# Gated blocks stored through ScalarE's DMA queue instead of SyncE's, in a language adapter with temporal gating

## The reference, cut to what matters

```python
# stage 0: adapter chosen by the sequence's language, residual, layer norm
h  = relu(x @ W1[lang] + b1[lang]);  a = h @ W2[lang] + b2[lang]
x1 = x + layernorm(x + a) * gamma0 + beta0
# stage 1
ctx    = causal_ema(x1, tau_ctx)                           # over positions
gated  = x1 * sigmoid(concat([x1, ctx]) @ Wg.T + bg)       # called g in the kernel
mod    = 0.5 + sigmoid(gelu(x1 @ Wn1.T + bn1) @ Wn2.T + bn2)   # 8 factors a position
traces = [causal_ema(gated * mod[..., d], tau[d]) for d in range(8)]
temporal = sum over d of traces[d] * softmax(blend)[d]
gate = sigmoid(temporal @ Wtemp.T + btemp)
soma = gelu(x1 @ Wsoma.T + bsoma)
out  = x1 + layernorm((soma * gate) @ Wout.T) * gamma + beta
```

## Time and profile before

| what | value |
|---|---|
| median of 3 runs | 1540.48 us (1540.35 to 1543.76) |
| the profiled execution: its time | 1546.37 us |
| its span | 1544.6 us |
| granted TensorE clock over the span | 0.988 |
| PE busy | 1430.2 us (93%) |
| DVE busy | 1004.6 us (65%) |
| ACT busy | 466.4 us (30%) |
| POOL busy | 398.0 us (26%) |
| DMA queue q1 (all DMAs of the program) | 184.97 MB, 41.0% of 16 engines |

### The profile page before, as it was taken

The page is one execution under the profiler, slowest core; times in us unless marked ns, Lnnn a source line. Parts: engine busy times, 40 slices in busy tenths (PEclk is TensorE's granted clock), DMA queues, the critical chain, the costliest instruction groups (busy, mean ns, idle before and its releaser), DMA issues.

```text
span 1544.6 us, 18784 instructions
## 1 busy us (share of the span) xinstructions
PE 1430.2 (93%) x7532; PEld 911.1 (59%) x7532; DVE 1004.6 (65%) x1421; ACT 466.4 (30%) x723; POOL 398.0 (26%) x294
## 2 busy tenths in 40 slices
PE   2899999999999999999899998999999999999986
PEld 1555756566575655756566575655756566575643
DVE  6866666765766666666765766666666765766362
ACT  2323332332323323332332332323332332333321
POOL 4304132240422304232230422304132140421102
PEclk8899999999999999999999999999999999999998
DMA  6471542616236261452516344271542616243150
GB/s 209 165 194 55 152 122 91 189 48 170 83 116 168 80 162 55 147 160 90 156 42 181 112 120 133 79 193 55 149 124 89 191 43 176 83 121 97 54 138 28
DMA packets 66137, 186.18 MB, mean 121 GB/s; under 512 B 9090, under 2 KB 13826, under 8 KB 53762
## 3 DMA queue, kind: packets, MB, share of 16 engines
q1 hardware_dynamic: 66050, 184.97, 41.0%
HBM read 134.61 MB, written 50.33 MB: 120 GB/s over the span
## 4 chain that ended last, share of the span: by engine, by line
PE 34%; DMA 28%; DVE 23%; SPq 5%; issue 4%; ACT 2%; POOL 1%; POOLq 0%; DVEq 0%
DMA g_spans<-g 21%; PE ring L784 20%; PE ring L791 12%; DVE U L694 9%; DMA grep<-g_spans 6%; DVE x L676 6%; SPq L308 5%; DVE U L667 2%; DVE seq_lo L621 2%; PE Tp L922 1%; PE Tp L912 1%; DVE g L706 1%; DVE V L712 1%; ACT g L460 1%; DVE g L702 1%
## 5 line engine op out<-in xcount | busy, mean ns | idle before, releaser
L694 DVE TENSOR_TENSOR U<-grep,w_qs 128x1024 f32<-128x1024 f32 x256 | 297.6, 1220 | 116.3 <-DMA grep<-g_spans 116.0
L363 POOL TENSOR_TENSOR x<-grep,b_row 128x512 f32<-128x512 f32 x64 | 83.3, 1333 | 673.2 <-DMA grep<-in_x 673.2
L784 PE MATMUL ring<-Wout,soma 128*128 128x512 f32 x512 | 222.5, 593 | 3.0 <-DVE soma L627 3.0
L912 PE MATMUL Tp<-U,Arep 128*32 128x256 f32 x2048 | 151.8, 389 | 46.8 <-DVE U L694 46.2
L784 PEld LDWEIGHTS ring<-Wout,soma 128*128 128x128 f32 x512 | 97.1, 190 | 125.3 <-issue 121.5
L372 POOL TENSOR_TENSOR grep<-grep,beta_row 128x512 f32<-128x512 f32 x64 | 79.7, 1277 | 223.0 <-DMA grep<-x_tiles 223.0
L702 DVE TENSOR_TENSOR g<-ring,bg_row 128x512 f32<-128x512 f32 x64 | 44.1, 689 | 142.5 <-PE ring L791 80.5
L627 DVE TENSOR_TENSOR soma<-ring,soma 128x512 f32<-128x512 f32 x64 | 43.9, 686 | 141.3 <-ACT ring L421 141.3
L460 ACT ACTIVATE g<-g 128x512 f32<-128x512 f32 x64 | 40.4, 632 | 303.1 <-DVE g L702 303.1
L912 PEld LDWEIGHTS Tp<-U,Arep 128*32 128x32 f32 x2048 | 49.8, 108 | 134.6 <-DVE U L694 90.7
L791 PE MATMUL ring<-seq_hi,Wtemp_hi 128*128 128x512 f32 x256 | 107.3, 419 | 15.1 <-DVE seq_lo L621 15.1
(11 more groups left out here) (138 smaller groups left out, 2538.5 us busy)
## 6 DMA issues: line engine op xcount, KB each, us to landing
grep<-g_spans SPq DMA_DIRECT2D x256, 256.0 KB, 4.9
grep<-in_xc SPq DMA_DIRECT2D x16, 1024.0 KB, 5.3
grep<-in_x SPq DMA_DIRECT2D x16, 1024.0 KB, 5.8
x_tiles<-x SPq DMA_DIRECT2D x16, 1024.0 KB, 4.0
g_spans<-g SPq DMA_DIRECT2D x64, 256.0 KB
grep<-x_tiles SPq DMA_DIRECT2D x16, 1024.0 KB, 4.8
out<-U SPq DMA_DIRECT2D x64, 256.0 KB, 2.0
W<-in_w SPq DMA_DIRECT2D x16, 256.0 KB, 7.3
```

Source lines behind the costliest of these rows:

```text
L363: nc.gpsimd.tensor_tensor(new[:, b, :], x_t[:, b, :], b2_row[:, :], ALU.add).then_inc(xb2_ready, 1)
L694: V_.tensor_tensor(U[:, (n + 2) % 4, :, :], grep[b % 2][:, :, at], w_qs[:, hh, at].unsqueeze(1).to_broadcast([P, NI, HC]), ALU.mult).then_ ...
L784: last = nc.tensor.matmul(dst, lhsT(n), rhs(n), start=(n == 0), stop=(n == steps - 1))
L912: last = nc.tensor.matmul(Tp[b % 2][i * L:(i + 1) * L, at], Arep[:, b * NI + i, hh, :], U[:, (n + 2) % 4, i, :], start=(hh == 0 and c == 0 ...
```

## The change

The function `store_spans` goes from SP's program to ACT's. ACT now issues the store of block b behind the sigmoid of block b (for block 0 behind the small sigmoid of `m_nat` as well), and waits for `g_ready` before it. SP keeps the loads in the same order, and their waits are what they were.

```diff
@@ SP, slot(k) @@
-                def store_spans(b):
-                    sp.wait_ge(g_ready, upto(4, k, b))
-                    sp.dma_start(g_dram[b].rearrange("s (i c) -> i s c", i=NI), g[:, b % 2, :]).then_inc(g_stored[b % 2], 16)
...
                 if has_cur:
-                    store_spans(0)
                     repeat_spans(0)
-                    store_spans(1)
                     repeat_spans(1)
-                    store_spans(2)
-                    store_spans(3)
                     repeat_spans(2)
                     repeat_spans(3)
@@ ACT, slot(k) @@
+                def store_spans(b):
+                    act.wait_ge(g_ready, upto(4, k, b))
+                    nc.scalar.dma_start(g_dram[b].rearrange("s (i c) -> i s c", i=NI), g[:, b % 2, :]).then_inc(g_stored[b % 2], 16)
...
                     nc.scalar.activation(m_nat, m_nat, ACT.Sigmoid).then_inc(msig_ready, 1)
+                    store_spans(0)
                     if k == 0:
                         split(4, 1, Wtemp[0][:, :, :])
                     for b in range(1, NB):
                         open_gate(b)
+                        store_spans(b)
                     soma_gelu(1)
```

## The result

The changed kernel takes 1545.4 us (median of 20 runs, 1540.3 to 1551.2). The kernel before takes 1541.7 us (median of 20 runs beside them, 1539.0 to 1546.4). The ratio is 1.0021, with a 95% interval of 1.0012 to 1.0030, so the change costs about 0.2%. The prediction had 1474 us and a range from 1464 to 1504. It was wrong.

The account below looks back on a forecast made before the run. Late stores in SP's queue, delaying loads of `grep`, were taken to bound the kernel. Cutting D from 12.28 to 8.1 saves 4.2 us a tile, 67 us over 16 tiles, giving 1474 us, range 1464 to 1504.

Parts of the forecast that it names:

- What bounds the kernel: In every tile DVE's products wait for loads of `grep`, held up by late stores in SP's queue: 116.0 us in all.
- D: Time in a tile from the end of block 0's products to the start of block 2's; mean 12.28 us before.
- Loads of block 2: D = 8.1: Block 2's loads start when block 0's products end; 6.9 us alone plus 1.2 for block 3's store beside them.
- What D loses, the tile loses, until PE becomes the limit.: Every us cut from D shortens the whole tile until PE limits it: 4.2 us a tile.
- PE's floor: PE's matmuls keep block 3's products from starting before 755.0, so D can't go below 7.8 us.
- Stores earlier: Stores of blocks 1 and 2 begin 2.9 and 4.4 us sooner; block 0's lands up to 2 us sooner, only slack.
- loads of block 1: Block 1's store lands between 731 and 734.3 beside block 0's loads; DVE starts block 1 some 2.4 us earlier, not counted.
- The bound of 743.9 us: Worst-case time for block 1's loads to be there, expected between 738 and 741.
- The stores take their engines in full turns: Rival, chance 0.27 with D up to 10.2: block 3's store delays block 2's loads fully; D 9.5, time 1496 us.
- Nothing comes of it: Rival, chance 0.04: same bytes on the same engines, so block 2's data comes when it came before; 1540 us.
- ACT: ACT's hold until block 3 is gated delays gelu and `trace(0)`, but some 6 us of cover make it cost nothing.

Follow-up runs that it names:

- e4: Changed kernel with g_spans laid out in the order of g's partitions, so stores are wide and loads read 2 KB rows: 1476.7 us, ratio 0.9565.
- e6: Kernel before, all stores still on SP, with g_spans in the order of g's partitions (wide stores): 1479.1 us, ratio 0.9583.
- e2: Kernel before with only block 2's store on ACT; blocks 0, 1 and 3 stored on SP, block 3 ahead of block 2's loads: 1534.6 us, ratio 0.9937.
- e3: Changed kernel with block 3's store back on SP, ahead of block 2's loads: 1560.0 us, ratio 1.0096 against the kernel before.
- e9: Changed kernel with the stores of blocks 0 and 1 back on SP, 2 and 3 on ACT: 1547.9 us, ratio 1.0042 against the kernel before.
- e12: Repeat of e6 (wide stores, all on SP), side by side with e11: 1480.7 us, ratio 0.9599 against the kernel before.
- e11: Repeat of e4 (wide stores, all on ACT), side by side with e12: 1478.3 us, ratio 0.9592 against the kernel before.
- e5: e4 with one unused row behind each 32, so stores are narrow again and loads keep 2 KB rows: 1536.1 us, ratio 0.9950 against the kernel before.
- e1: Kernel before with stores left on SP and only the four waits for gated blocks added on ACT: 1544.7 us, ratio 1.000.
- e7: Changed kernel with each store split into four DMAs of 32 partitions, layout and loads unchanged: 1490.1 us, ratio 0.9647 against the kernel before.

## Why the prediction was wrong, point by point

*What bounds the kernel.* Right about the place and wrong about the cause. The loads of `grep` end last, D was 12.3 us, and what the stretch loses the tile loses: e4's tile is 43.35 - 38.93 = 4.4 us shorter there, and 16 x 4.4 = 71 us is the 67 us that e4 gained (4.35% of 1541.7), within a few us. But the prediction took the late issue of block 2's store for a matter of queue order. e6 keeps the order and loses the lateness, so the cause was the width of the stores.

*Loads of block 2: D = 8.1.* The number was near, and its reason was wrong. D is 8.84, and 8.15 in the tile shown; the loads are issued when block 0's products end. For the store beside them the prediction added 1.2 us to 6.9, and the runs show 1.9. It took the 1.2 from the 299 GB/s, as a store's tail and loads moving together. The first row here counts the packets of that window, 748 to 749 of the kernel before. The second is a window of the changed kernel just before block 3's store moves any data, so with loads alone:

```profile
DMA packets 60, 0.30 MB, mean 299 GB/s; under 512 B 19, under 2 KB 19, under 8 KB 25
...
743.00:744.50 1.50, 1.50 (x6) 0.95 (x5) 0.00 (x0) 1.28 (x1) 0.00 (x0) 1.00 1.04 289
```

Only six of the 60 packets, 12 KB of the 0.30 MB, are 2 KB packets of the store, and loads alone reach 289 GB/s too. So that window said nothing of a store beside loads.

*"What D loses, the tile loses, until PE becomes the limit."* This is the step that failed. D gave 3.47 us a tile and the tile lost 0.4. The prediction took block 3's products to follow block 2's by 6.00 us or by PE's floor, and never worked out when block 3's loads can be issued. They wait for block 3's store. It had named this store as running beside block 2's loads, and charged the meeting only to the loads (1.2 us). Rows of before would have warned it. The gating of block 3 at 741.8, a store of 6.3 to 7.0 us and loads of 6.9 make 755.0 to 755.7 as an estimate, where block 3 was wanted at 741.2 + 8.1 + 6.0 = 755.3, so there was no slack for the store to lose. The runs show the opposite: of the store's 0.26 MB, 0.11 MB moved while the loads moved 1.02 MB, and it landed after 8.4 us. In the kernel before, the same store was ahead of block 2's loads in the queue, so block 3's loads could be issued straight behind them. The one order hid a store that the other exposes: 1.8 us at block 3's start and, with block 3 that late, 0.4 in its products (e2 and e3 take both away).

*Stores earlier, loads of block 1.* The prediction saw that block 1's store may take twice its time beside block 0's loads, and let block 1 pay. Block 0 paid, which the prediction had put at nothing: its loads were issued at 726.96 and DVE started at 736.79, 9.8 us later, where it had been 735.05 - 727.84 = 7.2. The slack ahead of `gate_logits(3)`, for which DVE had waited 0.81 us, took a part of that, and 1.7 us were lost (e2 and e9 take it away). Block 1's own start gained nothing: it comes 2.7 us after the end of block 0's products in the mean, before and after. Its loads had block 2's store beside them and took 9.4 us to DVE's start, where it was 6.8. The bound of 743.9 us that the prediction gave here has no working. Block 0's store was to land up to 2 us sooner. It took 6.3 us, from 720.62 to 726.94, and had taken 6.3 us before. Moving it off x1's queue gave nothing; that fits x1's store on the same engines, but no run tried it by itself. These are two rows of the chain and DVE's start in the kernel before, and two rows of the chain in the changed one:

```profile
721.50 6.32 DMA g_spans<-g
...
727.84 0.34 SPq L308
...
735.05 2.36 DVE L694 TENSOR_TENSOR U<-grep,w_qs 128x1024 f32<-128x1024 f32 x2 [0.35 <-DMA grep<-g_spans]
```

```profile
720.62 6.33 DMA g_spans<-g
...
726.96 0.33 SPq L304
```

*Rivals.* "The stores take their engines in full turns" was the nearest in mechanism, but it too priced only the delay of the loads. "Nothing comes of it", with 0.04, is what was measured. Its argument is nearest to what the runs show: with stores on four engines, what one transfer wins there another loses. I dismissed it by pointing at 12 idle engines, which is the very sign of the bound, since a load waits for all 16, and by calling queue order the cost, which e6 refutes. The Trainium skill says in the page "DMA: Bandwidth & Descriptors", section "Issuing engines are not separate DMA queues", that a second issuing engine saves only issue time. The runs agree: e12 and e11, the move with wide stores, differ by 2.4 us with overlapping intervals. In the same page of the Trainium skill, section "Why a DMA increments its semaphore by 16 and not by 1" (the prediction gave the section on queues), the number of engines follows from the outermost dimensions of the two sides. The trace agrees (0.26 of 16 engines for a dimension of 4), and the experiments e4 and e5 show what it is worth, 59 us. I had read that rule and used it only for a rate.

*ACT.* Right, in that it costs nothing. Counted from the gating of block 0, the gelu began 744.52 - 720.58 = 23.9 us later where it had been 740.94 - 721.47 = 19.5, and `trace(0)` 24.5 us where it had been 22.4. The lateness of block 0, 1.7 us, is in both. PE's waits for ACT are as short as before (some 2 us in the whole execution), and e1 shows no cost of the hold.

*PE as the floor.* Right as a bound on block 3's start, 755.0 - 741.2 = 13.8 us after block 0's products, and not reached in the changed kernel, where that is 16.6. e4 has 7.33 + 6.57 = 13.9 us. It is no floor of D, which is 7.33 in e4 and not 7.8 or more. That e4's 1476.7 us lie beside the forecast of 1474 doesn't bear the prediction out, since the change of e4 is another one; the 14.1 us that it forecast are those of a kernel with wide stores, on either queue (e6 has 14.2).

## What to carry to other kernels

Look at the width of a DMA before its place in a queue. A share of 0.26 with one transfer in flight means four engines of 16, and the cure is a layout or a split whose outermost dimension is wide. It was worth about 4% here, where the queue move by itself was worth nothing. When two transfers come to meet on the same engines, work out the landing of both and follow each landing to the next issue that waits for it, since the saving at one wait may be the price of the one after it. And idle engines beside a busy few are a bound when every load needs all of them.

## What the runs showed of the hardware

- **How two queues share an engine stays open.** In the 5.35 us of the windows above, ACT's queue moved 53 packets of 2 KB. SP's moved 189, of which some 124 carry data, 8 KB each, and the rest are small. If the loads are spread evenly over the 16 engines, the store's four engines moved some 0.25 MB of loads beside the 0.11 MB of the store; this is an estimate. With 2 KB rows on both sides (e5) the step from block 2 to block 3 was 6.8 us in place of 7.8, so the size of the rows seems to count. By what rule they take turns was not tried by itself.
- **TensorE's clock fell once behind a late block 3.** In the tile shown PE waited for block 3's products, and the granted clock then stood at half, its 1.2 GHz level, for some 7 us. These are windows of the changed kernel:

```profile
758.00:760.00 2.00, 0.80 (x5) 0.36 (x3) 0.88 (x1) 1.08 (x2) 0.00 (x0) 1.00 0.83 303
760.00:762.00 2.00, 1.10 (x16) 0.34 (x16) 2.00 (x3) 0.00 (x0) 0.48 (x1) 1.00 0.03 13
762.00:764.00 2.00, 1.83 (x16) 0.62 (x12) 2.00 (x2) 0.60 (x1) 2.00 (x2) 0.64 0.00 0
764.00:766.00 2.00, 1.12 (x9) 0.31 (x9) 2.00 (x4) 0.00 (x0) 2.00 (x2) 0.50 0.03 9
766.00:768.00 2.00, 2.00 (x4) 0.86 (x5) 1.15 (x2) 0.00 (x0) 2.00 (x2) 0.50 0.86 238
```

  PE had been busy 0.80 us of the two before 760 and 1.10 us of the next two, and the clock fell behind that. The rest of this tile was 51.3 us in place of 49.3. It was one tile of 15 here; the others with a late block 3 kept the clock, so lateness alone doesn't explain it. It may be why the runs of the changed kernel spread from 1540 to 1551, but that was not shown.
- **DVE's four products of block 3 took 5.70 us in place of 4.63** in six of the 16 tiles of the changed kernel. It is one product each time, with 2.29 us in place of 1.22. In all six, additions of the next tile's input on GpSimd (L355, from 761.52 in the tile shown) ran beside the whole of it, and beside none of the other products did GpSimd work for over 1.22 us. These six make the 0.44 us of the cuts. In the kernel before no product was slow; there block 3's came earlier. No run tried this by itself.
- **The loads of 2 KB rows were no slower than those of 8 KB.** The median from issue to landing in e4 is 4.6 us, as in e7, and with narrow stores the layout with the shorter rows gained 9 us (e5 against the changed kernel).
